# The first panel placed anew, and ScalarE's half of each second read issued after the rows queued ahead of SP's half

## The reference, cut to what matters

```python
h = relu(layernorm(x))                                # x is 5120 x 64
e_u = par_u[0]*par_u[1] * (diag_u[:, None] * h[:2048] @ W_u) + h[:2048]
e_i = par_i[0]*par_i[1] * (diag_i[:, None] * h[2048:] @ W_i) + h[2048:]
e = concatenate([e_u, e_i])
g = adj @ (adj.T @ e)                                 # adj is 5120 x 5120, float32, 105 MB
out = x + (g - mean(g)) / sqrt(var(g) + 1e-5) * gamma + beta + h
```

## Time and profile before

| what | value |
|---|---|
| median of 3 runs | 481.21 us (479.27 to 486.22) |
| the profiled execution, as timed | 485.2 us |
| its span in the profile | 483.4 us |
| TensorE busy, share of span | 411.6 us, 85% |
| VectorE busy | 391.4 us, 81% |
| ScalarE busy | 338.9 us, 70% |
| GpSimd busy | 28.7 us, 6% |
| granted TensorE clock, mean | 0.947 |
| moved by DMA | 139.42 MB, mean 288 GB/s |

### The profile page before, as it was taken

How to read it: one execution, slowest core, us unless ns; L and a number is a source line. 1 busy time by engine, 2 the same in 40 slices (tenths; PEclk the granted TensorE clock), 3 DMA queues, 4 the chain that set the end, 5 groups by cost and what they waited for, 6 DMA issues and landing times.

```text
span 483.4 us, 5124 instructions
## 1 busy us (share of the span) xinstructions
PE 411.6 (85%) x1948; PEld 156.9 (32%) x1948; DVE 391.4 (81%) x378; ACT 338.9 (70%) x426; POOL 28.7 (6%) x30
## 2 busy tenths in 40 slices
PE   0768929456999989999996999998799999697995
PEld 0423304312333324333332333233333333242332
DVE  4665999939899959989993998899299999849912
ACT  3447992394899379799573979938397993848433
POOL 1121700000000000000000000000000000001062
PEclk9989978696999999999998999999799999979999
DMA  7999657374988999999999899999999999969311
GB/s 240 405 408 406 226 195 230 128 316 119 318 298 308 394 306 384 319 316 362 406 351 276 342 269 289 373 406 330 258 353 298 311 405 403 304 134 183 56 59 50
DMA packets 63112, 139.42 MB, mean 288 GB/s; under 512 B 4208, under 2 KB 37488, under 8 KB 63088
## 3 DMA queue, kind: packets, MB, share of 16 engines
q1 hardware_dynamic: 45360, 123.28, 74.0%
q10 hardware_dynamic: 17728, 15.82, 12.5%
HBM read 137.78 MB, written 1.31 MB: 288 GB/s over the span
## 4 chain that ended last, share of the span: by engine, by line
PE 47%; DMA 26%; DVE 10%; ACT 8%; issue 6%; SPq 2%; ACTq 0%; DVEq 0%
PE h_ps L773 29%; DMA landing<-in_adj_dram 26%; PE tT_ps L715 14%; ACT kept L397 6%; DVE kept L569 4%; DVE kept L575 3%; PE tT_ps L723 1%; PE tr_ps L750 1%; PE tr_ps L705 1%; DVE tT_sb L590 1%; SPq L254 1%; SPq L276 1%; SPq L292 0%; PE h_ps L693 0%; ACTq L260 0%
## 5 line engine op out<-in xcount | busy, mean ns | idle before, releaser
L397 ACT ACTIVATE kept<-landing 32x1024 f32<-32x1024 f32 x257 | 271.2, 1055 | 21.9 <-PE h_ps L773 15.9
L715 PE MATMUL tT_ps<-landing,e_sb 128*64 128x512 f32 x768 | 182.9, 627 | 15.6 <-DMA landing<-in_adj_dram 15.6
L569 DVE COPY kept<-landing 32x1024 f32<-32x1024 f32 x207 | 147.0, 710 | 13.4 <-ACT kept L397 7.9
L773 PE MATMUL h_ps<-kept,t_quads 128*64 128x512 f32 x480 | 144.5, 606 | 0.0
L575 DVE STREAM_TRANSPOSE kept<-kept 128x2048 f32<-128x2048 f32 x60 | 134.0, 2280 | 3.2 <-ACT kept L397 2.8
L773 PE MATMUL h_ps<-landing,t_quads 128*64 128x512 f32 x240 | 108.4, 604 | 9.8 <-issue 9.8
L715 PEld LDWEIGHTS tT_ps<-landing,e_sb 128*64 128x64 f32 x768 | 56.3, 144 | 129.6 <-issue 106.9
L575 DVE STREAM_TRANSPOSE landing<-landing 128x2048 f32<-128x2048 f32 x30 | 67.4, 2288 | 4.8 <-DMA landing<-in_adj_dram 4.6
L773 PEld LDWEIGHTS h_ps<-kept,t_quads 128*64 128x64 f32 x480 | 45.2, 140 | 43.6 <-issue 43.1
L773 PEld LDWEIGHTS h_ps<-landing,t_quads 128*64 128x64 f32 x240 | 33.1, 139 | 56.4 <-issue 56.2
L407 ACT ACTIVATE kept<-tr_ps 128x512 f32<-128x512 f32 x40 | 21.9, 595 | 35.7 <-PE tr_ps L705 35.5
(11 more groups left out here) (61 smaller groups left out, 151.0 us busy)
## 6 DMA issues: line engine op xcount, KB each, us to landing
landing<-in_adj_dram SPq DMA_DIRECT2D x48, 2048.0 KB, 13.0
landing<-in_adj_dram SPq DMA_DIRECT2D x30, 512.0 KB, 12.1
landing<-in_adj_dram ACTq DMA_DIRECT2D x30, 512.0 KB, 13.1
kept<-in_adj_dram SPq DMA_DIRECT2D x2, 2048.0 KB, 24.8
x_sb<-in_x_dram SPq DMA_DIRECT2D x5, 256.0 KB, 8.1
out_dram<-x_sb SPq DMA_DIRECT2D x10, 128.0 KB, 1.8
kept<-in_L_gnn_W_u_dram SPq DMA_DIRECT2D x2, 16.0 KB, 4.6
kept<-in_L_gnn_W_i_dram SPq DMA_DIRECT2D x2, 16.0 KB, 3.9
```

Of the source, the lines that this page charges most:

```text
L397: last = nc.scalar.activation(dst, src, ACT.Copy)
L569: last = nc.vector.tensor_copy(dst, src)
L715: last = nc.tensor.matmul(tT_ps[half * D:(half + 1) * D, :], e_sb[:, g * RB + r, :], nat_rows(p, g)[:, r, half * BANK:(half + 1) * BANK], ...
L773: last = nc.tensor.matmul(h_ps[k][half * D:(half + 1) * D, :], t[:, b, :], tile, start=(p == 0 and b == 0), stop=True, skip_group_check=True)
```

## The change

- **Group 3 in the first panel** is turned by TensorE (as group 7 is) and no longer copied and turned by the move: KIND holds for the later panels, FIRST_KIND for the first. TensorE gets 32 transposes between its sums, ScalarE 8 copies of 128x512 for 9 of 32x1024, and VectorE loses 7 copies and two transposes. The copy out of PSUM now writes the row order of moved groups, with as many elements as before.
- **The normalising of x** gets five work slots for centred rows and five for squares instead of two and two, and its steps are interleaved by hand: squares of the next pairs go ahead of the root of this one, the copy of turned rows comes early, and copies of group 1 are put between one by one. All of x is read before natural 0.
- **VectorE, first panel**: copies of group 6 stand ahead of `take_tT(0)` instead of behind it, and the order is copies 1, 2, turn 1, copies 4, turns 2 and 4, copies 6.
- **GpSimd** adds beta in the tail, after the two small matrices, instead of early.
- **ScalarE's half of a second read** now first waits for the natural rows that stand just ahead of that read in LOADS: natural 2 for group 5, natural 3 for group 8, natural 9 for group 0. It also stands later: group 5 after 4 copies of the next panel's group 1, group 8 after the rest of these and 4 copies of group 2, group 0 after the first two tiles of group 7 and 4 copies of group 6. SP's half is issued as before. In the last panel the halves of 5 and 8 follow `move(4, 9)` as before, and what they wait for has landed long since.

```diff
+    FIRST_KIND = ("read", "move", "move", "turn", "move", "read", "move", "turn", "read", "move")
     KIND = ("read", "move", "move", "move", "move", "read", "move", "turn", "read", "move")
...
+        SCRATCH = (7, 4)
+        EGO = kept_slot(SCRATCH[0])
+        SQUARES = kept_slot(SCRATCH[1])
...
-            natural(0, 0)
             for u in range(2, PAIRS):
                 load_x(u)
-            for g in range(1, GROUPS):
+            for g in range(GROUPS):
                 natural(0, g)
...
-            pool.wait_ge(affine_in, 16 * 2)
-            for u in range(PAIRS):
-                pool.wait_ge(res_summed, u + 1)
-                pool.tensor_tensor(unit(x_sb, u), unit(x_sb, u), per_column(beta_sb[:, :]),
-                                   ALU.add).then_inc(res_ready, 1)
...
+            for u in range(PAIRS):
+                pool.wait_ge(res_summed, u + 1)
+                pool.tensor_tensor(unit(x_sb, u), unit(x_sb, u), per_column(beta_sb[:, :]),
+                                   ALU.add).then_inc(res_ready, 1)
...
             def second(p, g):
+
+                before = LOADS[LOADS.index((p, g, True)) - 1]
+                act.wait_ge(natural_in[before[1]], 16 * (before[0] + 1))
                 wait_landing_free(act, p, g, True)
                 load_second(act, p, g, range(NQ // 2, NQ))
...
+            squares(0)
+            squares(1)
+            root(0)
+            relu(0)
+            squares(2)
+            root(1)
+            egoT_copy(0)
+            relu(1)
+            squares(3)
+            root(2)
+            egoT_copy(1)
+            relu(2)
+            move(0, 1, 0, 1)
...
             move(0, 2)
-            move(0, 3)
-            move(0, 4)
+            turn_back(0, 3, 0)
+            turn_back(0, 3, 1)
+            move(0, 4, 0, 4)
+            turn_back(0, 3, 2)
+            move(0, 4, 4)
+            turn_back(0, 3, 3)
             second(0, READS[0])
...
                 move(p, 9)
+                if p < LAST:
+                    move(p + 1, 1, 0, 4)
                 second(p, READS[1])
                 if p < LAST:
-                    move(p + 1, 1)
+                    move(p + 1, 1, 4)
+                    move(p + 1, 2, 0, 4)
                 second(p, READS[2])
                 if p < LAST:
-                    move(p + 1, 2)
+                    move(p + 1, 2, 4)
                     move(p + 1, 3)
                     move(p + 1, 4)
+                    turn_back(p + 1, TURN, 0)
+                    move(p + 1, 6, 0, 4)
                     second(p + 1, READS[0])
-                    turn_back(p + 1, 0)
-                    move(p + 1, 6)
-                    turn_back(p + 1, 1)
+                    move(p + 1, 6, 4)
+                    turn_back(p + 1, TURN, 1)
...
             move(0, 1)
             move(0, 2)
             turn_moved(0, 1)
-            move(0, 3)
+            move(0, 4)
             turn_moved(0, 2)
-            move(0, 4)
-            turn_moved(0, 3)
             turn_moved(0, 4)
+            move(0, 6)
             take_tT(0)
...
+            sum_e(3)
+            turn_tiles(0, 3, 0)
+            sum_e(4)
+            turn_tiles(0, 3, 1)
+            sum_e(5)
+            turn_tiles(0, 3, 2)
+            sum_e(6)
+            turn_tiles(0, 3, 3)
+            sum_e(7)
+            turn_tiles(0, TURN, 0)
             sum_e(8)
+            turn_tiles(0, TURN, 1)
             sum_e(9)
```

More of the change, by code:

```diff
@@ L40, in gnn_layer_kernel @@
     EPS = 1e-5
+    FIRST_KIND = ("read", "move", "move", "turn", "move", "read", "move", "turn", "read", "move")
     KIND = ("read", "move", "move", "move", "move", "read", "move", "turn", "read", "move")
-    MOVES = tuple(g for g in range(GROUPS) if KIND[g] == "move")
     TURN = KIND.index("turn")
@@ L159, in turned_rows, with kind, of_kind @@
             return landing_slot(p, g, True) if KIND[g] == "read" else kept_slot(g)
+        def kind(p, g):
+            return KIND[g] if p else FIRST_KIND[g]
+        def of_kind(p, name):
+            return tuple(g for g in range(GROUPS) if kind(p, g) == name)
         def t_count(p, g):
@@ L164, in move_count, with tile_count @@
         def move_count(p, g):
-            return p * len(MOVES) + MOVES.index(g) + 1
-        def tile_count(p):
-            return p * BLOCKS
+            return sum(len(of_kind(q, "move")) for q in range(p)) + of_kind(p, "move").index(g) + 1
+        def tile_count(p, g):
+            return (sum(len(of_kind(q, "turn")) for q in range(p)) + of_kind(p, "turn").index(g)) * BLOCKS
         def read_count(p, g):
@@ L185, in wait_landing_free @@
                     eng.wait_ge(t_summed, t_count(p0, g0))
[L186 removed]
+                    if kind(p0, g0) == "move":
                         eng.wait_ge(moved_act, move_count(p0, g0))
                         eng.wait_ge(moved_dve, move_count(p0, g0))
[L189 to L190 removed]
+                    if kind(p0, g0) == "turn":
+                        eng.wait_ge(tr_filled, tile_count(p0, g0) + BLOCKS)
         def wait_kept_free(eng, p, g):
@@ L429, in take_blocks, with relu @@
                 nc.scalar.activation(t_blocks[:, :, :], rows64(tT_ps[:, :]), ACT.Copy).then_inc(blocks_ready, 1)
+            def relu(u):
+                act.wait_ge(normed, u + 1)
+                nc.scalar.activation(unit(e_sb, u), rows64(centred_work(u)), ACT.Relu).then_inc(ego_ready, 1)
             squares(0)
-            for u in range(PAIRS):
-                root(u)
-                act.wait_ge(normed, u + 1)
-                nc.scalar.activation(unit(e_sb, u), rows64(ego_work(u % 2)), ACT.Relu).then_inc(ego_ready, 1)
-                if u + 1 < PAIRS:
-                    squares(u + 1)
-                egoT_copy(u)
-                if 1 <= u < PAIRS - 1:
-                    move(0, 1, 3 * (u - 1), min(3 * u, ACT_MOVES[1]))
+            squares(1)
[10 more added lines that the diff above has]
+            move(0, 1, 0, 1)
+            squares(4)
+            root(3)
+            egoT_copy(2)
+            move(0, 1, 1, 2)
+            relu(3)
+            move(0, 1, 2, 3)
+            root(4)
+            egoT_copy(3)
+            move(0, 1, 3, 4)
+            relu(4)
+            move(0, 1, 4, 5)
+            egoT_copy(4)
+            move(0, 1, 5)
             for t, v in ((gamma_sb, gamma), (beta_sb, beta)):
@@ L498, in hT_copy @@
                 dst = work(4 + k % 2).rearrange("d (r q i) -> d r q i", q=NQ, r=RB)
-                kinds = [KIND[g] for g in BANKS[k]]
+                kinds = [KIND[g] == "read" for g in BANKS[k]]
                 if kinds[0] == kinds[1]:
@@ L606, in _ @@
             e_rows(0)
-            normalise(2)
-            for u in range(3, PAIRS):
-                e_rows(u - 2)
-                centre_x(u)
-                normalise(u)
-            e_rows(PAIRS - 2)
-            e_rows(PAIRS - 1)
+            norm(2).then_inc(normed, 1)
+            centre_x(4)
+            square_sum(3)
+            e_rows(1)
+            norm(3).then_inc(normed, 1)
+            square_sum(4)
+            e_rows(2)
+            norm(4).then_inc(normed, 1)
+            e_rows(3)
+            e_rows(4)
             move(0, 1)
@@ L756, in sum_h @@
                 for g in BANKS[k]:
-                    if KIND[g] == "turn":
+                    if kind(p, g) == "turn":
                         pe.wait_ge(blocks_ready, p + 1)
-                        pe.wait_ge(tr_emptied, tile_count(p) + BLOCKS)
-                    elif KIND[g] == "move":
+                        pe.wait_ge(tr_emptied, tile_count(p, g) + BLOCKS)
+                    elif kind(p, g) == "move":
                         pe.wait_ge(moves_turned, move_count(p, g))
@@ L787, in _ @@
             times_W(1)
-            for u in range(2, PAIRS):
-                sum_e(u - 2)
-                turn_ego(u)
-                times_W(u)
-            for g in range(PAIRS - 2, TURN):
-                sum_e(g)
-            turn_tiles(0, 0)
-            sum_e(TURN)
-            turn_tiles(0, 1)
+            sum_e(0)
+            turn_ego(2)
+            times_W(2)
+            sum_e(1)
+            turn_ego(3)
+            times_W(3)
+            sum_e(2)
+            turn_ego(4)
+            times_W(4)
+            sum_e(3)
[8 more added lines that the diff above has]
+            turn_tiles(0, TURN, 0)
             sum_e(8)
+            turn_tiles(0, TURN, 1)
             sum_e(9)
```

97 lines of the change are left out of this document (48 added, 49 removed).

## The result

The changed kernel takes 503.73 us, the median of 4 runs (502.01 to 511.07), beside 483.72 for the kernel before (4 runs, 479.27 to 487.94) on the same chip. The ratio is 1.0448 [1.0334, 1.0561], 95% interval in brackets: slower, where 465 with a range up to 480 was forecast. The profiled execution of after (511.07, span 508.9) is over 1.5% above the fastest of its kernel and, like all such executions, left out of the ratio, so of the 25.5 us between its span and the 483.4 before, some 4 are its own (the ratio stands for 21.7).

What follows compares the result with a forecast made beforehand. VectorE was taken to bound the first part and, after the change, the middle panels. Gains of 9.3 (first part), 6.8 (intervals) and 0 (tail), together 16.1, took 481.2 to 465 us, range 451 to 480.

Steps and rivals of the forecast that it cites:

- First panel: Start of the kernel up to `take_tT(0)`: forecast to end at 80.0 instead of 89.3 us, 9.3 earlier.
- the normalising: First panel, TensorE's five products waiting for ScalarE's copies of turned rows: gain between 0 and 9.5 us, taken as 3.
- H: Mark in each panel: end of bank (0,1) of h, which frees group 1's kept slot and starts the next panel's copies.
- the upper bound: Tail: GpSimd's moved additions were taken to cost nothing, at most 8.55 us if uncovered.
- VectorE as the limit of a middle panel: Middle panels: VectorE, not TensorE, ends the panel, 33.7 us after L8, at H + 62.7.
- T: Mark in each panel: start of `take_tT`, the end of the next panel's first product; middle panels forecast at H + 62.7.
- L8: Landing of group 8's half in a middle panel: forecast H + 29, between H + 24.5 and H + 33.5.
- the half's time: Middle panels, transfer of group 8's half after its issue: 11.2 to 15.7 us plus a start of 1 to 2.
- Rival 3: Middle panels: group 8's half lands too late, L8 = H + 37.5, T = H + 71.2, 498.6 us; chance 0.07.
- break-even: Middle panels: the loss cancels the first part's gain at T = H + 65.8, L8 = H + 32.1.
- Natural 9: Middle panels: without group 0's half beside it, lands 5.3 us earlier, about H + 53.5; TensorE's 4.2 + 1.9 go.
- Rival 2: Middle panels: order of the same bytes gives nothing, L8 = H + 31, 472 to 477 us, say 474; chance 0.24.

Runs made afterwards that it cites:

- the issues alone: The kernel before with only ScalarE's three new waits and later issue places, no new first panel: 524.06 us, ratio 1.0744.
- wait 8: The changed kernel with the new wait kept only for group 8's half (for natural 3): 491.53 us, ratio 1.0169.
- late places: The changed kernel without new waits, halves of groups 5 and 8 placed still later among ScalarE's copies: 485.51 us, ratio 1.0054.
- no wait: The changed kernel with the new waits removed and the later places kept: 470.14 us, ratio 0.9677.
- the last stage: Last of seven stages of a load-only test without computation: natural rows with ScalarE's half of a second read beside them, 17.1 us.
- wait 0: The changed kernel with the new wait kept only for group 0's half (for natural 9): 469.22 us, ratio 0.9708.
- The fastest kernel: The changed first panel with old issues for groups 5 and 8, group 0's half late without its wait: 458.13 us, ratio 0.9466.
- waits 5 and 8: The changed kernel with the waits of groups 5 and 8 kept and only group 0's dropped: 489.80 us, ratio 1.0120.
- the kernel with this wait alone on the old issues: The changed first panel with old issues for groups 5 and 8, group 0's half late with its wait: 467.51 us, ratio 0.9653.
- the waits of 5 and of 0: The changed kernel with one new wait kept: group 5's alone 473.17 us, ratio 0.9789; group 0's alone 469.22 us, ratio 0.9708.

## Why the prediction was wrong

**First panel: right, and somewhat too small.** VectorE began its copies at 41.8 (43.0 forecast), so the normalising gave 4.2 and not 3. Its copies took 9.8 as taken, TensorE waited 5.25 for ScalarE's tiles near 50 us (5.7), and `take_tT(0)` came at 78.9 (80.0), 10.4 sooner for the 9.3 forecast. The 33.3 up to the first H, taken as unchanged, became 31.5. GpSimd's additions in the tail cost nothing (53.8 to 53.8), as taken, against the 8.55 of the upper bound: they take 6.2 there, and two of VectorE's transposes beside them still take 4.51. Other kernels' tails lie between 53.8 and 59.0, and that of the issues alone, without the additions, is 55.5.

**VectorE as the limit of a middle panel: right.** T = L8 + 33.7 held where the halves are late: in after, wait 8, late places and no wait, 74.4 - 40.7, 68.5 - 34.9, 69.5 - 35.7, 61.4 - 27.8 give 33.7, 33.6, 33.8, 33.6, and the other two middle panels of each give the same within 0.2.

**L8: the step that failed.** The prediction put it at H + 29, within 24.5 and 33.5; it measured 40.7, 39.3 and 44.8. Two terms were mis-sized.

The first is the wait's own time. I let natural 3 land at H + 12.5 and the issue follow. It landed at H + 17.6, 16.3 and 20.1, no sooner than the 15.9 to 17.8 before, though ScalarE's half no longer stood beside it at the start. SP's half of group 5 is ahead of it in the queue and, without its partner, moved 194 GB/s (I had read 240 from a stretch in which 43 of the 480 packets were the partner's); natural 3 came 8.4 to 9.2 after that, near the 7.9 that I had taken. What moved was the start: natural 2 had landed at H + 1.6, 2.1 and -1.3 before, so group 5's wait could not let its half go at H + 0.5, and in after both natural 2's landing and that issue came at about H + 4.2, 2.6 and 4.2. With the wait of group 8 alone natural 3 does let the half go at H + 13.1, 13.6 and 12.4, near my 12.5, and L8 is still H + 34.9, 36.1 and 33.8: this first term is not enough without the second.

The second, and the larger, is the half's time. I took 11.2 to 15.7, and 1 to 2 for a start. It needed 23.1, 23.0 and 24.7 from issue to landing, and the trace before already had it: the half issued at H + 3.6 landed at H + 23.1, 24.6 and 22.5, some 20 after. I reckoned from rates where a duration stood in the trace. With queues otherwise short the rates were not wrong: the half beside natural rows took 13.5 in the last stage. In late places, with group 5's half down or nearly so and no partner, it took 18.4, 18.6 and 16.8, some 3.5 of them before its first packet, where I had 1 to 2. In after 4.6 to 5.5 us of group 5's half are still ahead of it in ScalarE's queue as well. Counted from the landing of ScalarE's half of group 5:

| kernel | group 5's half lands, after H | group 8's half, after that |
|---|---|---|
| before | 13.3, 6.9, 8.2 | 9.8, 17.7, 14.4 |
| no wait | 15.3, 14.9, 15.9 | 12.5, 11.7, 12.9 |
| wait 0 | 15.6, 15.2, 15.9 | 12.5, 12.3, 11.6 |
| wait 8 | 17.4, 17.7, 16.1 | 17.5, 18.4, 17.6 |
| late places | 17.2, 18.8, 16.5 | 18.5, 17.1, 17.6 |
| after | 22.4, 20.9, 25.6 | 18.3, 18.4, 19.2 |

Where it is issued early it needs 10 to 14 behind group 5's, and where it is issued as natural 3 lands 17 to 19. (The 17.7 of before's second middle panel is an exception; there SP's half of group 5 landed last, at H + 11.0, and it is 13.6 behind that. The fastest kernel, issued early too, has 16.1 in its last interval, which I can't explain.) What goes with the difference is the partner. SP's half of group 8 starts as natural 3 ends; the wait lets ScalarE's go only then, its first packets come some 5 us later, and ahead of them is what is left of group 5's. In the panel shown, SP had started 1972 of the 2048 packets of its two halves (of groups 5 and 8) by 213 us, and ScalarE 1011, all of them of group 5's 1024. It then ran without its partner, beside natural 4 (277 packets to 343 from 215 to 220 us) or nearly alone at 177 GB/s. That the partner, and not something else that comes with a late issue, makes the difference between 12 and 18 is argued. And its end is ragged; the queues from 225 to 233 us (packets, MB, share):

```profile
q1 hardware_dynamic: 604, 2.41, 91.1%
q10 hardware_dynamic: 127, 0.12, 5.0%
```

The last 0.12 MB of the half's 1.05 take the last 8 to 9 us ahead of its landing at 233.9. That a few engines are behind and share packet for packet with natural rows is how I read it; the trace's packets don't name their engine, so it stays argued.

**Rival 3 is what happened, and beyond its numbers.** It had the half behind group 5's and one for one beside natural rows, L8 = H + 37.5 and 498.6 us. I gave it 0.07 because VectorE's turn of 8 had been fed at H + 22.9 before; that said nothing of a half issued 14 us later. Its break-even, L8 = H + 32.1, fits: waits 5 and 8 with L8 near H + 35.5 come out at 1.012 [1.0005, 1.0236], above before and by less than 2%.

**Natural 9: right in the mechanism, and outweighed.** With ScalarE's half issued only 5 to 7 us ahead of its landing, natural 9 lands at H + 53.6 to 55.8 in the middle panels of the kernel without waits (forecast 53.5; 58.2 to 60.0 before). In after it lands at H + 66 to 72, since everything ahead of it is late. The cost at the end of the wait was overlooked too: I had ScalarE's copies end ahead of T, but in the kernel with this wait alone on the old issues they end after it (169.2 against 167.2).

**Rival 2, that order gives nothing: wrong.** The same bytes took between 458 and 504 us by order alone, with one first panel. The Trainium skill (DMA: Bandwidth & Descriptors, "Issuing engines are not separate DMA queues") says that several issuers save only time at the sequencer. The measurement agrees for one side (12.1 and 12.4 us) and not for two (8.95 against 11.6 from one queue with the sides in turn), where it decides: what counts is which partitions the queues write at a time.

**The ends of the range.** By the prediction's own terms the sum runs from 449 (L8 = H + 24.5, first part 12) to 482 us (L8 = H + 33.5, first part 6.3), not from 451 to 484. The measured time lies outside either, so this changes nothing in the outcome.

Open are what the ragged end has of the 23 us, the pair of waits 0 and 8 without 5, why the first H moved 2 us closer, and why the same first panel ends between 75.7 and 78.9 us in different kernels.

## What to carry to other kernels

Before a transfer is made to wait for another, look at what it runs beside now: here the two halves of a read used different partitions and were fast only together, so an order that kept the same bytes lost a third of the rate or more (319 to 206 GB/s by itself, 322 to 194 in the kernel). Take a transfer's time as issue to landing from a row of the trace where the queues are as full as they will be, not as bytes over a rate. And where a late start was wanted here, a later place in the order of an engine that is never idle gave it (0.947 for group 0's half) without what a wait puts behind itself (0.965).

## What the runs showed of the hardware

- **Two queues that write partitions 0 to 63 and 64 to 127 at the same time** move 319 GB/s, and 206 to 219 when one side is written at a time, by one queue or two. Within the kernel this was worth 17 us of 483.
- **A transfer issued on ScalarE's queue while SP's is full of natural rows** sends its first packet 3.5 to 5.4 us after the issue (late places and after, middle panels), in the stages with short queues 1.0 to 1.9.
- **Waits can be free one by one and dear together**: the waits of 5 and of 0 cost nothing alone, yet the three together cost 18 us of interval and some 16 of time more than those of 5 and 8 (1.0448 against 1.0120).
- **VectorE's copies beside GpSimd's additions** take 14.72 us instead of 9.80, its transposes beside them 4.51 for two, as without.
